# Value products of local attention over all 128 rows, with zeros beside each block of probabilities

## The reference, cut to what matters

```python
def local_attention(q, k, v):                 # w = 32, nw = n // w
    bk2, bv2 = (look(bk), look(bv))           # window before + own window: 64 keys
    sim = jnp.einsum('bhwie,bhwje->bhwij', bq, bk2) * QK_SCALE
    sim = jnp.where(mask, -jnp.finfo(sim.dtype).max, sim)
    attn = jax.nn.softmax(sim, -1)
    out = jnp.einsum('bhwij,bhwje->bhwie', attn, bv2)
    return out.reshape(b, h, n, d)

def attn_layer(x, Wqkv, qs, ksc, Wo):
    q, k, v = jnp.split(x @ Wqkv, 3, -1)      # then l2norm, scales, rotary tables
    ...
    out = local_attention(q, k, v)
    return out.transpose(0, 2, 1, 3).reshape(b, n, INNER) @ Wo

for i in range(DEPTH):                        # 6
    x = attn_layer(shift_tokens(x), ...) + x
    x = ffn_layer(shift_tokens(x), ...) + x
```

## Time and profile before

| | us |
|---|---|
| median of 3 runs (lowest to highest) | 4470.26 (4465.94 to 4483.92) |
| the profiled execution | 4469.34 |
| its span, first to last instruction | 4467.4 |
| TensorE, matmuls busy | 3989.5 |
| ScalarE busy | 3119.9 |
| VectorE busy | 2987.1 |
| GpSimd busy | 2763.5 |

### The profile page before, as it was taken

The page is one execution under the profiler, slowest core; times in us unless marked ns, Lnnn a source line. Parts: engine busy times, 40 slices in busy tenths (PEclk is TensorE's granted clock), DMA queues, the critical chain, the costliest instruction groups (busy, mean ns, idle before and its releaser), DMA issues.

```text
span 4467.4 us, 213887 instructions
## 1 busy us (share of the span) xinstructions
PE 3989.5 (89%) x91104; PEld 3089.1 (69%) x91104; DVE 2987.1 (67%) x4910; ACT 3119.9 (70%) x10376; POOL 2763.5 (62%) x2582
## 2 busy tenths in 40 slices
PE   6888885999998999989999989999899999899998
PEld 3555554777757777757777567777477776577784
DVE  6788774677746776657767557667467765577664
ACT  5877784777746777747777567777477776577774
POOL 4667675666636676546766466666366665566661
PEclk9999997999999999999999999999999999999999
DMA  0000002111111111111111111111111111111110
GB/s 33 2 2 2 2 2 67 42 42 42 44 49 39 44 44 41 39 50 42 44 41 42 47 42 47 40 41 39 52 42 41 42 41 57 33 44 42 44 39 27
DMA packets 100282, 168.87 MB, mean 38 GB/s; under 512 B 26224, under 2 KB 33648, under 8 KB 99056
## 3 DMA queue, kind: packets, MB, share of 16 engines
q1 hardware_dynamic: 99312, 154.89, 11.7%
HBM read 26.13 MB, written 2.10 MB: 6 GB/s over the span
## 4 chain that ended last, share of the span: by engine, by line
PE 55%; issue 13%; POOL 11%; DVE 3%; ACT 1%; POOLq 0%; DMA 0%; SPq 0%; DVEq 0%; ACTq 0%
PE s_bank L1172 10%; PE s_mix L1245 7%; PE s_bank L1258 7%; PE s_bank L1193 6%; POOL s_rotated L804 5%; POOL s_sq L826 4%; PE s_mix L1152 4%; PE s_proj L1217 3%; PE s_proj L1218 3%; PE s_proj L1219 3%; POOL s_probs L813 2%; DVE s_qk L786 2%; PE s_mix L1205 2%; PE s_mix L1204 2%; PE s_mix L1206 2%
## 5 line engine op out<-in xcount | busy, mean ns | idle before, releaser
L804 POOL TENSOR_TENSOR s_rotated<-s_rotated,s_by_sin 128x512 f32<-128x512 f32 x768 | 1161.2, 1533 | 377.2 <-DVE s_by_sin L1082 377.2
L902 ACT ACTIVATE s_probs<-s_bank,s_neg_max 128x64 f32<-128x64 f32 x3072 | 931.8, 335 | 11.6 <-DVE s_neg_max L1023 11.6
L813 POOL TENSOR_TENSOR s_probs<-s_probs,s_rden 128x256 f32<-128x256 f32 x768 | 497.0, 648 | 567.1 <-DVE s_rden L1030 563.8
L1172 PE MATMUL s_bank<-s_qk 32*32 32x64 f32 x49152 | 626.5, 223 | 145.8 <-issue 144.7
L1172 PEld LDWEIGHTS s_bank<-s_qk 32*32 32x32 f32 x49152 | 525.0, 103 | 266.0 <-issue 264.6
L902 ACT ACTIVATION_READ_ACCUMULATOR s_probs<-s_bank,s_neg_max 128x1 f32 x3072 | 704.3, 229 | 0.0
L893 ACT ACTIVATE s_probs_t<-s_mix 128x512 f32<-128x512 f32 x384 | 229.9, 599 | 666.3 <-PE s_mix L1152 666.3
L1077 DVE TENSOR_TENSOR s_rotated<-s_proj,s_cos 128x1024 f32<-128x1024 f32 x384 | 470.3, 1225 | 328.0 <-ACT s_sq L934 328.0
L786 DVE TENSOR_TENSOR s_qk<-s_rotated,s_inv_norm 128x1024 f32<-128x1024 f32 x384 | 680.5, 1772 | 0.0
L826 POOL TENSOR_TENSOR s_sq<-s_sq 128x512 f32<-128x512 f32 x384 | 511.1, 1331 | 85.1 <-ACT s_sq L934 61.6
L1193 PE MATMUL s_bank<-s_sq,s_same_head 128*128 128x256 f32 x1536 | 428.6, 403 | 126.9 <-POOL s_sq L826 123.1
(11 more groups left out here) (120 smaller groups left out, 8140.7 us busy)
## 6 DMA issues: line engine op xcount, KB each, us to landing
s_v<-s_v SPq DMA_DIRECT2D x384, 192.0 KB, 2.5
s_v<-s_v SPq DMA_DIRECT2D x384, 64.0 KB, 3.5
s_qk<-f_wqk SPq DMA_DIRECT2D x6, 1024.0 KB, 5.5
s_xs_raw<-u SPq DMA_DIRECT2D x48, 128.0 KB
s_xf<-u SPq DMA_DIRECT2D x48, 128.0 KB, 2.3
s_xs_raw<-u SPq DMA_DIRECT2D x48, 127.8 KB
s_xf<-u SPq DMA_DIRECT2D x48, 127.8 KB, 2.6
s_qk<-f_wv SPq DMA_DIRECT2D x6, 512.0 KB, 6.0
```

What stands on the lines that cost most here:

```text
L804: nc.gpsimd.tensor_tensor(rotated[:, par, :, half, :], rotated[:, par, :, half, :], by_sin[:, :, 1 - half, :], (ALU.subtract, ALU.add)[half])\
L813: nc.gpsimd.tensor_tensor(part, part, by, ALU.mult).then_inc(S["probs_done"], 1)
L902: last = nc.scalar.activation(probs[:, par, h, b, :], score_bank[h][:, b * KEYS:(b + 1) * KEYS], ACT.Exp, scale=-1.0, bias=neg_max[:, par, ...
L1172: last = nc.tensor.matmul(score_bank[e][to:to + WIN, w * KEYS:(w + 1) * KEYS], qk[rows, quad % 2, 0, c, WIN + at:WIN + at + WIN], qk[rows, ...
```

## The change

- `probs_t` has one more axis of two. The transposed probabilities of rows 0 to 63 go to its place 0, those of rows 64 to 127 to place 1; the rest of the tensor is set to zero once, at the start of the stage.
- A value product covers all 128 rows and 64 columns of `v`, and 64 columns of `probs_t` (32 queries of one window, 32 of the other): 16 matmuls of the source in a step, where there were 32 with 64 rows and 32 columns. The two tiles differ in their columns alone. All go to one bank, `vy_bank`; `tr_bank` is a bank of its own for the transposes.
- The copy of the transposed probabilities is two: ScalarE rows 0 to 63 (`pt_first`), VectorE rows 64 to 127 (`pt_second`), the latter between the minima and the write of queries and keys.
- The transposes wait for both copies of the step before and no longer for `y_done`; the value products wait for both copies of their own.
- The result's copy reads one bank straight.
- In step 3, `tokens_high` is the first work of ScalarE's step, and `tokens_rest` stands ahead of GpSimd's normalisations.

```diff
-        mix_ps = st.enter_context(nc.psum_tensor("s2_mix", [P, 2, 512], F32))
-        bank = [st.enter_context(nc.psum_tensor(f"s2_bank{i}", [P, 512], F32)) for i in range(4, 8)]
+        bank = [st.enter_context(nc.psum_tensor(f"s2_bank{i}", [P, 512], F32)) for i in range(2, 8)]
+        ss_bank, score_bank, tr_bank, vy_bank, wo_bank = bank[0], bank[1:3], bank[3], bank[4], bank[5]
...
-        probs_t = sb("s2_probs_t", [P, 2, NT, HPG, WIN])
+        probs_t = sb("s2_probs_t", [P, 2, NT, HPG, 2, WIN])
...
+            pool.memset(probs_t[:, :, :, :, :, :].rearrange("p e t h a q -> p (e t h a q)"), 0.0).then_inc(S["consts"], 1)
...
+                if p == XS_STEP and s < NSEQ - 1:
+                    tokens_rest(s + 1)
                 if live(s, p, LAG_SCORE, first):
                     normalise(0)
                     normalise(1)
-                if p == XS_STEP and s < NSEQ - 1:
-                    tokens_rest(s + 1)
...
-                    nc.scalar.activation(probs_t[:, :, :, :, :].rearrange("p e t h q -> p (e t h q)"), tr_bank, ACT.Copy)\
-                      .then_inc(S["pt_done"], 1)
+                    nc.scalar.activation(probs_t[0:KEYS, :, :, :, 0, :].rearrange("p e t h q -> p (e t h) q"),
+                                         tr_bank[0:KEYS, :].rearrange("p (n q) -> p n q", q=WIN), ACT.Copy)\
+                      .then_inc(S["pt_first"], 1)
...
+                if p == XS_STEP and s < NSEQ - 1:
+                    tokens_high(s + 1)
                 if ln and p == LN_STEP + 2:
                     inverse_std(f)
...
-                    nc.scalar.activation(y[:, place(p, LAG_VALUE)[2], :, :]
-                                         .rearrange("p x (t a z) -> p a (x t) z", t=NT, a=2),
-                                         mix_ps[:, :, 0:2 * TOKS // 2].rearrange("p a (b z) -> p a b z", z=2 * WIN),
-                                         ACT.Copy)\
+                    nc.scalar.activation(y[:, place(p, LAG_VALUE)[2], :, :],
+                                         vy_bank[:, :].rearrange("p (a t) -> p a t", a=2), ACT.Copy)\
...
+                if live(s, p, LAG_VALUE, first):
+                    m = n - LAG_VALUE
+                    if not (first and p == LAG_VALUE):
+                        dve.wait_ge(S["pv_done"], m)
+                    dve.wait_ge(S["tr_done"], m + 1)
+                    nc.vector.tensor_copy(probs_t[KEYS:P, :, :, :, 1, :].rearrange("p e t h q -> p (e t h) q"),
+                                          tr_bank[KEYS:P, :].rearrange("p (n q) -> p n q", q=WIN))\
+                      .then_inc(S["pt_second"], 1)
...
-                        pe.wait_ge(S["pt_done"], m)
-                        pe.wait_ge(S["y_done"], m)
+                        pe.wait_ge(S["pt_first"], m)
+                        pe.wait_ge(S["pt_second"], m)
...
-                    pe.sem_inc(S["pv_inputs"], 1)
+                    mixed = vy_bank[:, :].rearrange("p (x t a e q) -> p x t a e q", x=2, t=NT, a=2, e=2)
                     for pair in range(2):
                         for t in range(NT):
                             for e in range(2):
-                                for a in range(2):
-                                    for h in range(2):
-                                        head = 2 * pair + h
-                                        rows, at = slice(a * KEYS, (a + 1) * KEYS), ((quad % 2) * HPG + head) * HD
-                                        to = ((pair * NT + t) * 2 + e) * WIN
-                                        last = nc.tensor.matmul(
-                                            mix_ps[HD * h:HD * (h + 1), a, to:to + WIN],
-                                            v[rows, cols, (half * NT + t) * 2 + e, at:at + HD],
-                                            probs_t[rows, e, t, (head + e) % HPG, :], start=True, stop=True,
-                                            tile_position=(a * KEYS, HD * h))
+                                for h in range(2):
+                                    head = 2 * pair + h
+                                    at = ((quad % 2) * HPG + head) * HD
+                                    last = nc.tensor.matmul(
+                                        mixed[HD * h:HD * (h + 1), pair, t, :, e, :],
+                                        v[:, cols, (half * NT + t) * 2 + e, at:at + HD],
+                                        probs_t[:, e, t, (head + e) % HPG, :, :], start=True, stop=True,
+                                        tile_position=(0, HD * h))
```

More of the change, by code:

```diff
@@ L600, in build_stage2 @@
         proj_ps = st.enter_context(nc.psum_tensor("s2_proj", [P, 2, 2, TOKS], F32))
-        mix_ps = st.enter_context(nc.psum_tensor("s2_mix", [P, 2, 512], F32))
-        bank = [st.enter_context(nc.psum_tensor(f"s2_bank{i}", [P, 512], F32)) for i in range(4, 8)]
-        ss_bank, score_bank, wo_bank = bank[0], bank[1:3], bank[3]
-        tr_bank, vy_bank = mix_ps[:, 0, :], mix_ps[:, 1, :]
+        bank = [st.enter_context(nc.psum_tensor(f"s2_bank{i}", [P, 512], F32)) for i in range(2, 8)]
+        ss_bank, score_bank, tr_bank, vy_bank, wo_bank = bank[0], bank[1:3], bank[3], bank[4], bank[5]
         up_bank = [tuple(proj_ps[:, i, :, :].rearrange("p a t -> p (a t)") for i in range(2)),
-                   (score_bank[0][:, :], score_bank[1][:, :]), (tr_bank, vy_bank)]
+                   (score_bank[0][:, :], score_bank[1][:, :]), (tr_bank[:, :], vy_bank[:, :])]
         w_high = sb("s2_w_high", [P, QUADS * 4 * P + INNER], F32R)
@@ L665, in build_stage2 @@
                  "add_done ss_done guard_done log_done inv_done norm_done score_done max_done exp_done "
-                 "rden_done probs_done tr_done pt_done v_mm v_done v_moved0 v_moved1 v_moved2 v_moved3 pv_inputs pv_done y_done wo_done attn_res "
+                 "rden_done probs_done tr_done pt_first pt_second v_mm v_done v_moved0 v_moved1 v_moved2 v_moved3 pv_done y_done wo_done attn_res "
                  "xf_in f_mean f_xc f_sq f_var f_log f_rstd f_xn f_xa f_up f_gate f_hid f_down ffn_res "
@@ L795, in _ @@
             pool.memset(ln_shift[:, :], 0.5 * float(np.log(LN_SCALE))).then_inc(S["consts"], 1)
-            pool.wait_ge(S["consts"], 3)
+            pool.wait_ge(S["consts"], 4)
             def step(l, s, p, first):
@@ L865, in _ @@
         def _(act):
-            act.wait_ge(S["consts"], 3)
+            act.wait_ge(S["consts"], 4)
             def centred_square(f):
@@ L955, in step @@
                                          bias=ln_shift[:, 0:1]).then_inc(S["inv_done"], 1)
-                if p == XS_STEP and s < NSEQ - 1:
-                    tokens_high(s + 1)
             def ffn_gate(f):
@@ L988, in _ @@
               .then_inc(S["cast"], 1)
-            dve.wait_ge(S["consts"], 3)
+            dve.wait_ge(S["consts"], 4)
             dve.wait_ge(S["cast"], 2)
@@ L1119, in _ @@
             pe.wait_ge(S["const_in"], 48)
-            pe.wait_ge(S["consts"], 3)
+            pe.wait_ge(S["consts"], 4)
             pe.wait_ge(S["cast"], 2)
@@ L1203, in step @@
                     toks, cols = slice(p % TILES * P, (p % TILES + 1) * P), slice(p // TILES * (INNER // 2), (p // TILES + 1) * (INNER // 2))
-                    nc.tensor.matmul(vy_bank, xs_high[:, s % 2, toks], wv[0][:, cols], start=True, stop=False)
-                    nc.tensor.matmul(vy_bank, xs_high[:, s % 2, toks], wv[1][:, cols], start=False, stop=False)
-                    nc.tensor.matmul(vy_bank, xs_rest[:, s % 2, toks], wv[0][:, cols], start=False, stop=True)\
+                    nc.tensor.matmul(vy_bank[:, :], xs_high[:, s % 2, toks], wv[0][:, cols], start=True, stop=False)
+                    nc.tensor.matmul(vy_bank[:, :], xs_high[:, s % 2, toks], wv[1][:, cols], start=False, stop=False)
+                    nc.tensor.matmul(vy_bank[:, :], xs_rest[:, s % 2, toks], wv[0][:, cols], start=False, stop=True)\
                       .then_inc(S["v_mm"], 1)
@@ L1227, in step @@
                     cols = quad // 2
-                    pe.wait_ge(S["pt_done"], m + 1)
+                    pe.wait_ge(S["pt_first"], m + 1)
+                    pe.wait_ge(S["pt_second"], m + 1)
                     if full:
```

2 lines of the change are left out of this document (1 added, 1 removed).

## The result

| us | before | after |
|---|---|---|
| median (lowest to highest) | 4475.48 (4465.94 to 4483.92), 4 runs | 4181.77 (4167.27 to 4189.79), 4 runs |
| profiled execution | 4469.34 | 4182.92 |
| span | 4467.4 | 4181.1 |
| mean granted clock | 0.977 | 0.986 |

The ratio is 0.934, with a 95% interval of 0.931 to 0.937. The change saves 294 us where the prediction had 181; the time lies 43 us under its range.

The account below looks back on a forecast made before the run. TensorE was taken as the bound, delayed by GpSimd's sum of squares at the head norms and by instruction fetches in the score products. 4469.3 - 131 - 75 + 0 + 25 = 4288 us; 8-in-10 range 4225 to 4440.

Parts of the forecast that it names:

- The tokens' rounding in step 3: GpSimd's sum of squares no longer waits for the rounding, shortening TensorE's wait at the head norms: 131 us gained.
- rival E: Step 3's move does nothing, as the tokens' DMA is late or GpSimd's normalisations become last: 4420 us, chance 0.03.
- the term's 21 us: Part of the rounding's 131 us: half the slow-clock time of the step behind the wait, over 42 steps.
- The value block: Value products, half as many pairs with twice the streamed columns: 1.07 us a step, unchanged, so 0.
- B: In the value products load and stream run one behind the other: block 1.5 us, total 4428 us, chance 0.14.
- C: Every value-product load waits for the stream ahead on the same rows: block 1.9 us, 4534 to 4576 us, chance 0.07.
- the prediction's sum: A value-product round costs the longer of load and stream: 54 against 27 ns before, 54 against 53 after.
- The copies: ScalarE's copy stays 0.60 us; VectorE's new one, 261 us in all, is hidden in its waits: cost 0.
- Rival D: VectorE or ScalarE becomes the bound, steps stay about 8 us, the fetch's gain is lost: 4370 us, chance 0.09.
- Fewer instructions: 64 of 450 TensorE instructions a step go, so fetch stalls at the score products shrink: 75 us gained, between 0 and 150.
- my lengths: Estimated stall lengths by packet border position, value to score products: mean 0.51 us a step before, 0.30 after.
- What shorter steps give back: Layer norm work in steps 5 to 7 shows more and the fetch gets less ahead: 25 us lost, between 0 and 80.

Follow-up runs that it names:

- e1: Kernel before with only the tokens' rounding moved in step 3, value products left at 64 rows by 32 columns: 4348.34 against 4469.52 us, 0.973.
- e6: Changed kernel with each value product cut in two, 32 columns of probs_t at a time, twice as many matmuls: 4494.95 against 4477.42 us, 1.004.
- e7: Changed kernel with VectorE's copy of 64 rows made twice, first into a spare tensor: 4191.38 against 4477.42 us for the kernel before, 0.936.
- e8: Kernel before with the two band products ahead of the score products made five times each: 4559.06 against 4472.57 us, 1.019.
- e5: Changed kernel with 32 tiny matmuls added each step between the band products, directly ahead of the score products: 4515.9 us, 1.008 to the kernel before.
- e10: Changed kernel with 32 tiny matmuls once ahead of the layer loop, moving all packet borders a quarter packet: 4180.04 against 4462.5 us, 0.936.
- e9: Changed kernel with the four transposes between the two halves of the score products instead of behind them: 4266.17 against 4472.57 us, 0.954.

## Why the prediction was right in its parts and wrong in its size

*The tokens' rounding in step 3: right.* Forecast 131 us. Transposes, norms and projections lost 136 us, in e1 alone 142, with e1's total 121 lower (rival E, that the move does nothing, had 0). The wait at the norms fell to 37.9 us, not under 25, and the half clock's time by more than the term's 21 us (88 us of the 207, worth half of that).

*The value block: right, 0.* It took 415.2 us and takes 418.5. Rivals B (1.5 us a step) and C (1.9) are refuted: 1.09. e6 shows that the stream does not set the round; that the load of 64 columns does is the reading that fits the prediction's sum, not the only one. The Trainium skill, "TensorE: Matmul & The Clock Gate", Part 3, lets a load overlap matmuls in flight only in another row group; here both tiles have all rows, and the overlap is complete (58 ns a round, not 107).

*The copies: right, 0.* VectorE's 266.7 us are hidden, and 267 more in e7 cost 10. TensorE did wait for the new copy, but 6 times, 4.7 us in all. Rival D, a bound of VectorE or ScalarE, did not come: steps without a stall take 7.3 us, in sequence 7 too, where they took 8.07 and 7.32. Queue 8's packets (644 for 640) and the mean clock (0.986, above 0.985) are as forecast. From the changed kernel's lines by form, the prices that did grow lie on engines with room:

```profile
L783 DVE TENSOR_TENSOR s_qk<-s_rotated,s_inv_norm 128x1024 f32<-128x1024 f32 x384 | 743.8, 1937 | 11.5
...
L1047 DVE COPY s_probs_t<-s_bank 64x512 f32<-64x512 f32 x384 | 266.7, 695 | 29.6 <-PE s_bank L1157 18.2
```

*Fewer instructions: the step that failed.* "Gain 0.2 x 384 = 75 us, between 0 and 150": the score products gained 157 us, and the stalls inside them 160. The mechanism held. Thin work in the way (e8, e6) takes the stalls away with more instructions in the step, dense work right ahead (e5) brings them back, and it is a matter of time at a border of 256 instructions, not of their number. What was mis-sized is the stall time that remains: 0.09 us a step (35.4 / 384), where my lengths gave 0.30. They took a packet as there 3.65 to 3.8 us behind the last border (2.95 + 0.7, 3.3 + 0.5), so that every border reached sooner is a stall. The table shows the two parts of the error: borders under 3 us fell to 39 to 78 of 151, which the lengths had in kind (128 positions to 68), and of those that were left only 36 to 59% stalled, where before nearly all did. Stalls behind more than 4 us, 51 before, which the lengths did not have at all, fell to 6 to 13.

What else decides there I could not settle. In the changed kernel no border stalled whose last two packets together took over 9 us (0 of 149), in e10 4 of 150, in the kernel before 38 of 111; so the last packets' time is not the whole of it, and how far TensorE's queue had run ahead at that point is not in the trace.

*What shorter steps give back: 25 us forecast, none seen.* The two halves add up to 280 us of the 294.

*The range.* The sum's own bounds reached lower than the range did: with the upper 150 for the fetches and nothing given back it is 4469.3 - 131 - 150 = 4188 us. I cut the range at 4225 as if the terms' ends could not meet, and two did.

## What to carry to other kernels

A block of tiny matmuls can be bound by the fetch of its own instructions: look for gaps put down to "issue" inside it, on the same pairs in one pass of a loop after another, and price them by how soon each packet border is reached, since 64 instructions fewer of 450 in a step took away four fifths of the stalled time here. A product whose time stays the same with half the streamed columns (e6) takes a second operand block for nothing, zeros included, and so halves the instructions at no cost. When each term of a sum has bounds, the range must reach to where the likely ones meet.

## What the runs showed of the hardware that was not expected

- A fetch of 16 KB is 256 TensorE instructions, and a stalled border is passed a median 2.4 us before and 2.5 us after the change behind the start of queue 8's last transfer (5 to 95%: 2.2 to 3.0 and 2.3 to 3.3). The Trainium skill, "Runtime: NRT & Kernel Launch", section "Instruction fetch mechanics", has the 256 too and calls the crossing mostly hidden; here the stalls in the score products take 196 us of 4467.
- VectorE and ScalarE read two halves of one PSUM bank's rows side by side at no cost: 695 ns for VectorE and 591 for ScalarE, both in the 306 steps in which the copies ran together for over 0.4 us and in those in which they ran apart; a full bank took 682.
- GpSimd's token rest beside VectorE's write took 2.34 us where it took 1.34 in its old place, and VectorE's write a mean 1937 ns where it had 1772; the sampled step took 7.35 us all the same.
- 335 us more of thin TensorE work cost 87 us (e8): the fetch and the wait for GpSimd ran on beside it.
- A further change of TensorE's tile shape costs some 0.17 us: 127 us for 768 more of them, in the score products, transposes and norms of e9 together, stalls left out.
